# Expert tiles: gathers for the tile two steps ahead issued before the accumulating transfers

## What is computed

```python
def _L0_ffn_ref(x, router_w, gate_w, gate_b, up_w, up_b, down_w, down_b):
    router_logits = xf @ router_w.T
    probs = jax.nn.softmax(router_logits, axis=-1)
    topv, topi = jax.lax.top_k(probs, TOP_K)
    ...
    g = jnp.einsum('nd,edf->nef', xf, gate_w) + gate_b
    u = jnp.einsum('nd,edf->nef', xf, up_w) + up_b
    h = jax.nn.silu(g) * u
    expert_out = jnp.einsum('nef,efd->ned', h, down_w) + down_b
    y = jnp.einsum('ne,ned->nd', probs, expert_out)
```

## Time and profile before

| | us |
|---|---|
| median of 3 runs | 1502.59 (1501.65 to 1505.24) |
| the profiled execution, its own time | 1504.22 |
| its span, first to last instruction | 1502.5 |
| PE busy | 1328.1 (88%) |
| DVE busy | 839.2 (56%) |
| ACT busy | 930.4 (62%) |
| POOL busy | 799.8 (53%) |
| granted TensorE clock, mean | 0.94 of full speed |
| expert stage, POOL's first to last instruction | about 1040 to 1471 |

### The profile page before, as it was taken

How to read it: one execution, slowest core, us unless ns; L and a number is a source line. 1 busy time by engine, 2 the same in 40 slices (tenths; PEclk the granted TensorE clock), 3 DMA queues, 4 the chain that set the end, 5 groups by cost and what they waited for, 6 DMA issues and landing times. The chain is left out here.

```text
span 1502.5 us, 31115 instructions
## 1 busy us (share of the span) xinstructions
PE 1328.1 (88%) x10439; PEld 1124.5 (75%) x10439; DVE 839.2 (56%) x1799; ACT 930.4 (62%) x2096; POOL 799.8 (53%) x885
## 2 busy tenths in 40 slices
PE   5899999999999999999778999952499999998680
PEld 4788888888888888888566777741388888888680
DVE  3344554444455554545448888848565555656454
ACT  4677777777777777777515777740055565655453
POOL 2234444434444444444517777720458888887863
PEclk9999999999999999999888999985599999999895
DMA  3300000101000000000122444322346656665647
GB/s 133 79 16 22 29 30 23 30 15 29 23 30 29 23 29 15 29 16 23 62 68 60 107 109 109 96 71 67 96 113 164 151 147 150 152 154 135 179 89 231
DMA packets 137125, 117.71 MB, mean 78 GB/s; under 512 B 46594, under 2 KB 121962, under 8 KB 137002
## 3 DMA queue, kind: packets, MB, share of 16 engines
q1 hardware_dynamic: 122026, 95.51, 20.9%
q0 software_dynamic: 14976, 20.62, 7.9%
HBM read 79.89 MB, written 33.58 MB: 76 GB/s over the span
## 5 line engine op out<-in xcount | busy, mean ns | idle before, releaser
L294 POOL TENSOR_SCALAR_AFFINE_SELECT a_decay<-a_decay 128x256 f32<-128x256 f32 x256 | 114.7, 452 | 257.9 <-ACT a_decay L374 256.3
L497 DVE TENSOR_TENSOR a_probs<-a_ps_s,a_decay 128x384 f32<-128x384 f32 x256 | 131.7, 553 | 158.2 <-PE a_ps_o L677 147.4
L303 POOL TENSOR_TENSOR a_key_sum<-a_probs 128x256 f32<-128x256 f32 x128 | 94.3, 736 | 170.4 <-DVE a_probs L497 158.4
L337 ACT ACTIVATE a_qk_exp<-a_ps_qk 128x512 f32<-128x512 f32 x128 | 76.5, 598 | 137.0 <-PE a_ps_qk L583 130.1
L1796 POOL DMA_INDIRECT sum_rows<-e_y_out,e_target x78 | 125.1, 1604 | 47.4 <-ACT e_y_out L1851 20.2
L583 PE MATMUL a_ps_qk<-a_xT_hi,a_w_hi 128*128 128x256 f32 x512 | 145.0, 283 | 3.6 <-ACT a_qk_relu L338 3.6
L583 PE MATMUL a_ps_qk<-a_xT_hi,a_w_lo 128*128 128x256 f32 x512 | 144.1, 281 | 0.0
L583 PE MATMUL a_ps_qk<-a_xT_lo,a_w_hi 128*128 128x256 f32 x512 | 143.9, 281 | 0.0
L490 DVE SCALAR_TENSOR_TENSOR a_qk<-a_qk_exp,a_qk_relu 128x512 f32<-128x512 f32 x128 | 89.1, 696 | 94.5 <-ACT a_qk_relu L338 94.4
L658 PE MATMUL a_ps_s<-a_qk 64*128 64x256 f32 (+1 forms) x1024 | 131.4, 337 | 0.7 <-DVE a_probs L497 0.4
L372 ACT ACTIVATE a_decay<-a_ps_c,a_c_now 128x256 f32<-128x256 f32 x256 | 124.3, 486 | 2.0 <-PE a_ps_c L648 1.4
(11 more groups left out here) (295 smaller groups left out, 4021.9 us busy)
## 6 DMA issues: line engine op xcount, KB each, us to landing
e_gu_raw<-in_L_ffn_gate_w SPq DMA_DIRECT2D x23, 512.0 KB
e_gu_raw<-in_L_ffn_up_w SPq DMA_DIRECT2D x23, 512.0 KB
e_dn_raw<-in_L_ffn_down_w SPq DMA_DIRECT2D x23, 512.0 KB
a_x_in<-in_x SPq DMA_DIRECT2D x16, 256.0 KB
a_x_res<-in_x SPq DMA_DIRECT2D x16, 256.0 KB, 2.8
x_rows<-a_x SPq DMA_DIRECT2D x16, 256.0 KB, 2.2
x_bo_rows<-a_x_bo SPq DMA_DIRECT2D x16, 256.0 KB, 2.2
b_x_in<-x_rows SPq DMA_DIRECT2D x16, 256.0 KB, 3.1
```

Of the source, the lines that this page charges most:

```text
L294: pool.affine_select(out=d, in_=d, compare_op=ALU.is_ge, fill=0.0, base=0, pattern=[[0, 2], [1, P]], channel_multiplier=-1)\
L303: pool.tensor_tensor(key_sum[:], probs[:, :, P:N], probs[:, :, N:TRI], ALU.add).then_inc(keys_summed, 1)
L497: vec.tensor_tensor(probs[:, h, :], ps_s[h][:, 0:TRI], decay[h][:], ALU.mult)\
```

## The change

On POOL, in the body of one tile, the gathers for tile t+2 come before the accumulating transfers of tile t-1 instead of behind them. Nothing is added or removed, and no other engine's program differs.

```diff
             def tile(t, par, turn):
                 if has(t, 1):
                     low_parts(1 - par, turn + par)
+                if has(t, 2):
+                    gather_rows(t + 2, par, turn + 1)
                 if has(t, -1):
                     add_rows(t - 1, 1 - par, turn - 1 + par)
-                if has(t, 2):
-                    gather_rows(t + 2, par, turn + 1)
```

## The result

The changed kernel takes 1533.9 us (median of 4 runs, 1527.2 to 1538.3) against 1502.6: 1.020 times as long, with an interval of 1.018 to 1.022. The direction of the prediction came true, the size did not: +31.3 us instead of +12.1, and above the range (1499 to 1521).

What follows compares the result with a forecast made beforehand. PE was taken to set the big tiles' pace, with POOL nearly as full. Start +2.7, big rounds +12.7 and end -3.3 made +12.1 us, so 1514.7 us against 1502.6, range 1499 to 1521.

Steps and rivals of the forecast that it cites:

- The wait that comes forward: POOL, ahead of the gathers: DVE's share is held to the subtractions' end, so POOL waits 1.23 us for the list.
- The round: POOL's twelve big-tile rounds: 18.8 us each instead of 17.74, bounds 17.53 and 19.27, in all +12.7 us.
- The start: Up to POOL's subtractions for tile 3: these begin later than 1128.36, +2.7 us.
- The end: Seven rounds, tile 15 to 22: waits from late gathers go, an index wait stands in each; 99.3 us, -3.3 us.
- The later accumulating transfers: Transfers of tile t-1, some 6 us later in the end tiles: costed at nothing unless landing takes over half a round.
- Clock: PE in the big tiles: waits might bring its clock below full speed, which would add to the forecast; no size given.
- The faster one: POOL never waits for the list, as DVE gets in between two subtractions: -10.8 us, 1491.8 us, chance 0.14.
- The half wait: Only the index cast is held, gathers keep 4.84 us; POOL waits 0.84 us: +1.9 us, 1504.5 us, chance 0.18.

Runs made afterwards that it cites:

- Run 1: Changed order, with DVE's cast of the target list moved to the head of its tile, against the changed kernel: 1520.8 us.
- run 3: Changed order, with DVE's target cast and index cast both moved to the head of its tile, against the changed kernel: 1490.1 us.
- run 5: Changed order, casts where they were, with a semaphore between each two of POOL's four subtractions, against the changed kernel: 1508.8 us.
- run 2: Changed order, with DVE's index cast alone moved to the head of its tile, against the changed kernel: 1509.1 us.

## Why the prediction was right on the big tiles' mechanism and wrong on the small tiles

**The wait that comes forward: right.** POOL waits for DVE's index cast ahead of nearly all gathers, and PE for `hidden(2)`, 1.2 to 1.6 us a big tile. POOL's wait was put at 1.23 and is 1.30 to 1.40, once 1.62: the index cast ends 0.43 us behind the subtractions (forecast 0.42), the way from the cast to the gather is 0.97 in the tile shown instead of 0.81.

**The round: right in kind, taken too low.** 18.8 was taken between 18.6 and 19.27; it is 19.28, at the upper bound. That bound came from the one row in which gathers directly followed an index cast; I took it for a single slow case. They now follow the cast in every tile, and take 5.06 to 5.39 us (5.28 in the tile shown, 1234.94 to 1240.22). What is left of the difference is for the most part the wait, some 0.1 us longer than put. This term was 5.8 us too small. The rows also show what goes with the slow gathers: behind the index cast and `hidden(2)` DVE takes the low parts of the hidden values (`e_hid_lo`, line 1945), and the gather of 1.27 us begins inside one of these. From tile 3 on, the 36 gathers of after that begin inside an `e_hid_lo` take 1.05 to 1.37 us, the 26 others 0.94 to 1.00. So the new place behind the list is also a place beside these subtractions; the last section says more, but no run tests it. The start came out at +3.2 (forecast 2.7, its bounds 2.4 to 3.1).

**The end: wrong; this is the step that failed.** The prediction took one index wait of 1.23 us for each of the seven small rounds, 99.3 us, and nothing behind the last. It had the row that mattered, a target cast of 4.35 us beside subtractions, but used it only to show that DVE can be blocked, and asked of the share alone whether it falls into the subtractions. It named the other outcome too, the cast of 0.32 us at 1408.28, "where POOL had been idle before its subtractions", and did not draw the conclusion that after the change POOL would no longer be idle there. Three of the seven rounds hold the target cast and last 16.08, 16.09 and 16.05 us instead of 12.6, which takes the 99.3 to 109.7 of the 110.1 measured, and the stretch behind, where the next casts are held, is 5.0 us longer. Run 1 moves the target cast out of the subtractions and changes nothing else: its small tiles need 100.16 us, the 99.3 of the sum nearly, and its 1520.8 us lie just inside the range.

**The price of a held instruction** is not the time that it is held but what stands behind it. Behind the share that is the second share, the index cast and `hidden(2)`; behind the target cast it is the rows out of psum, their scaling and the cast of the next rows on ACT, and only then the low part, the shares and the index cast.

**The later accumulating transfers** were put at nothing, and that held: in after POOL waits for the landing of none of them from 1125 to 1480.

**Clock: no part of it in the big tiles.** It stays at 1.00 there. In the small tiles it is 0.88 against 0.93 in the same stretch of before, with more waits between PE's work, and 0.93 again in run 1. PE is busy there for 86.78 us against 86.46, and in the 4.57 us between the held cast and the gather shown above (1430.40 to 1434.97) PE works for 0.31 us, so its clock has no part in that chain. I charge nothing to it.

**The rivals.** The faster one (1491.8: POOL never waits for the list) did not happen, but run 3 made it so: the same order with the lists early gives 1490.1. There the casts stand elsewhere. Its own condition, that DVE gets in between two subtractions, is what run 5 made: POOL's wait went in ten of twelve big rounds, but with the gaps these still took some 18.3 us, and the time was 1508.8. The half wait (1504.5) did not happen.

## What to carry to other kernels

When a step is moved onto an engine's critical round, go through every instruction of the engine that shares something with it and ask where it will stand in the new timing, not only the one that collides in the trace of before. A short instruction that can be held by a neighbour (here a cast of four columns) is priced by the chain queued behind it; make such lists early, or make them where nothing holds them. Before hoisting transfers on a full engine, see what else can be moved off it: the same change cost 31 us with the subtractions on GpSimd and won 14 with them on VectorE, where GpSimd had room and nothing was held.

## What the runs showed of the hardware

**The hold can last over several of GpSimd's instructions.** Beside four subtractions without a gap VectorE's cast took 5.49 us; with a semaphore between them (run 5) a held instruction ended with the subtraction that it met, after 0.7 to 1.3 us, or 2.1 to 2.6 where it came ahead of the first one. The Trainium skill (SBUF — State Buffer, Who interferes with whom) has the lock held for the whole instruction. With gaps that is what run 5 shows; without them the traces show it held over four. An idle stretch ahead of the four has the same effect as the gaps: where GpSimd had been idle for 0.40 us or more, one of them alone held a cast or a share (1.11 us in run 2, 0.32 in the earlier trace rows); where it had been idle for 0.03 us or less, the hold went to the end of the last. This is so in every trace of this case that has the four on GpSimd without gaps. Why was not tried. Nor does any run show why in after a cast that came 0.69 us ahead of the subtractions' recorded start (1456.30), beside the last transfer, was held to their end as well, 6.27 us.

**VectorE instructions with psum as one of two inputs were not held.** Within the subtractions shown first (1227.94 to 1233.54), DVE's `e_xT_lo` (line 1896), which subtracts an SBUF operand from psum, keeps the 1.29 us that it also takes in before at 1240.65, beside no subtraction of GpSimd:

```profile
1229.63 1.29 DVE L1896 TENSOR_TENSOR e_xT_lo<-e_ps_x,e_xT_hi 128x512 fp32r<-128x512 f32 x2 [2.17 <-ACT e_xT_hi L1831]
```

**It works the other way round too.** In run 3 POOL's transfers are stretched when they begin while DVE subtracts two SBUF operands (POOL's and DVE's timelines):

```profile
1242.12 1.58 POOL L1796 DMA_INDIRECT sum_rows<-e_y_out,e_target  x1 [0.30 <-issue]
1244.01 2.38 POOL L1796 DMA_INDIRECT sum_rows<-e_y_out,e_target  x1 [0.30 <-issue]
...
1242.35 1.47 DVE L1947 TENSOR_TENSOR e_hid_lo<-e_hid,e_hid_hi 128x512 fp32r<-128x512 f32 x2
1243.73 1.22 DVE L1914 TENSOR_TENSOR e_dn_lo<-e_dn_raw,e_dn_hi 128x1024 fp32r<-128x1024 f32 x1
```

The one that begins inside `e_dn_lo`, with 0.94 us of it left, takes 2.38 us instead of 1.56; the one before it begins ahead of the `e_hid_lo` and takes its usual 1.58. From tile 3 on in run 3 every accumulating transfer of 1.66 us and more (up to 2.42) begins inside such a subtraction and is longer by what is left of it less 0.1 to 0.2 us. The others, but for one, begin outside or with less than that left, and take 1.54 to 1.63. This is read from the traces; no run moved DVE's subtractions away. Rounds of POOL in run 3 are up to 18.7 us long for this, while PE, which does not wait for it there, keeps its 17.54.
